# A cross-attention kernel: Wkv split by column halves in turn with the first context block, and x normalised behind the third piece

## Chip, cores and metric

The kernel runs on one core of one Trainium2 chip. The metric is device microseconds of one execution; the median of several runs is compared. The profile is that of one execution of its own.

## What is computed

A block of a perceiver on x (8 x 64 x 512) and a context (8 x 1601 x 512): cross-attention, a second attention whose values are taken on the diagonal, and a mixture of eight experts. The change touches only the start of the cross-attention. Its reference, cut:

```python
q = (x @ Wq + bq).reshape(B, N, H, hd).transpose(0, 2, 1, 3)
kv = (ctx @ Wkv + bkv).reshape(B, K, 2, H, hd).transpose(2, 0, 3, 1, 4)
k, v = (kv[0], kv[1])
attn = jnp.einsum('bhnd,bhkd->bhnk', q * SCALE, k)
attn = jax.nn.softmax(attn, axis=-1)
out = jnp.einsum('bhnk,bhkd->bhnd', attn, v)
...
return out @ Wproj + bproj
...
x = x + _L0_xattn_ref(_layernorm(x, axis=-1), ctx_1024, ...)
```

## The kernel before

Every engine's program is written out by hand and in order; they wait for each other with semaphores alone. A product in single precision is made of three: each operand is split into a high part (ScalarE copies it to fp32r, names in `_hi`) and a low part (VectorE subtracts the high part from the whole, `_lo`), and TensorE adds high x high, high x low and low x high in one bank (function `three`, lines 151 to 153). A "piece" is one bank of keys or values, 12 such matmuls over the four quarters k of the 512 rows of Wkv.

A unit works on half the context of one batch (a chunk of 7 or 6 tiles of 128 rows). While it attends, it makes the keys and values of the next unit. The first unit has nothing to attend to, and its preparation stands by itself ahead of the loops; the change lies there. It runs as follows.

SyncE issues all loads on one queue: the first four tiles of context (`raw0`, 1 MB), four quarters of Wkv of 512 KB (each with a semaphore of its own, `wkv_in0` to `wkv_in3`), the bias of the keys `bkc` (2 KB, semaphore `bk_in`), x, Wq, the bias of q, and three more tiles of context. The next load of context waits for `turned` to be 4, the one behind it for 12.

TensorE turns the context in four quarters (line 693, semaphore `turned`), waits for all of `cT_lo` (`turn_lo`) and all of `Wkv_lo` (`wkv_lo`), and makes eight pieces (n = 0 to 7: four of keys, four of values) in three banks in rotation. From n = 3 on each waits until VectorE has split the piece that was in its bank (`kv_lo`). Behind n = 4 and 5 it turns the normalised x (`turn_x`, line 706, waits for `ln_done`), behind n = 6 and 7 the second part of the context (line 665); then it makes q in four pieces (waits for `wq_lo`), then seven more pieces with turns of the next chunk. q is split, written to DRAM and read back by heads before the first scores (line 756).

ScalarE's and VectorE's orders match: four quarters of context, four quarters of Wkv (full width, 1024 columns), pieces 0 and 1, the normalisation of x (VectorE has the statistics, `norm_vector`, lines 113 to 139; ScalarE the square root in between, `norm_scalar`), pieces 2 and 3, Wq, and so on. A keys' piece is two instructions on each engine, a values' piece one. Both engines wait for `bk_in` ahead of their first copy. The argument `between` of `norm_vector` puts other work into VectorE's wait for the root.

Of the kernel before, what the change touches and what calls it, by code (L numbers as in the profile page):

```python
# [24 lines left out]
def perceiver_kernel(nc, x_in, ctx_in, Wq, bq, Wkv, bkv, Wproj, bproj,  # L25
                     WQ, WK, WVd, WVu, Wg, bg, W1, b1, W2, b2, out):
    B, S, D = x_in.shape
# [36 lines left out]
    with ExitStack() as whole:  # L64
# [241 lines left out]
        def program(block):  # L306
# [93 lines left out]
            def _(act):  # L400
# [25 lines left out]
                def first_kv_hi(n):  # L426
                    kv_hi(n, first_kv_bank(n), 0, n)

                act.wait_ge(sem("bk_in"), 16)
                for k in range(KC):  # L430
                    first_ctx_hi(k, 0, 0, k)
                for k in range(KC):
                    act.wait_ge(sem(f"wkv_in{k}"), 16)
                    nc.scalar.copy(Wkv_hi[:, k, :], Wkv_raw[:, k, :]).then_inc(sem("wkv_hi"), 1)
                first_kv_hi(0)
                first_kv_hi(1)
                norm_scalar(act, 1, lnt1)
                first_kv_hi(2)
                first_kv_hi(3)
                act.wait_ge(sem("wq_in"), 16)  # L440
# [6 lines left out]
                first_kv_hi(4)  # L447
                x_hi(0)
                x_hi(1)
                first_kv_hi(5)  # L450
                x_hi(2)
                x_hi(3)
                first_kv_hi(6)
                first_ctx_hi(2 * KC + 0, 0, 1, 0)
                first_ctx_hi(2 * KC + 1, 0, 1, 1)
                first_kv_hi(7)
# [58 lines left out]
            def _(dve):  # L515
# [32 lines left out]
                dve.wait_ge(sem("bk_in"), 16)  # L548
                for k in range(KC):
                    first_ctx_lo(k, 0, 0, k)  # L550
                for k in range(KC):
                    dve.wait_ge(sem("wkv_hi"), k + 1)
                    nc.vector.tensor_tensor(Wkv_lo[:, k, :], Wkv_raw[:, k, :], f32(Wkv_hi[:, k, :]), ALU.subtract) \  # L553
                        .then_inc(sem("wkv_lo"), 1)
                first_kv_lo(0)
                first_kv_lo(1)
                dve.wait_ge(sem("x_in"), 16)
                norm_vector(dve, 1, x_tok, x_tok, lnt1)
                first_kv_lo(2)
                first_kv_lo(3)  # L560
                dve.wait_ge(sem("wq_hi"), 1)
                nc.vector.tensor_tensor(Wq_lo[:, :, :], Wq_raw[:, :, :], f32(Wq_hi[:, :, :]), ALU.subtract) \
                    .then_inc(sem("wq_lo"), 1)
# [6 lines left out]
                first_kv_lo(4)  # L570
                x_lo(0)
                x_lo(1)
                first_kv_lo(5)
                x_lo(2)
                x_lo(3)
                first_kv_lo(6)
                first_ctx_lo(2 * KC + 0, 0, 1, 0)
                first_ctx_lo(2 * KC + 1, 0, 1, 1)
                first_kv_lo(7)
# [77 lines left out]
            def _(pe):  # L657
# [53 lines left out]
                pe.wait_ge(sem("turn_lo"), KC)  # L711
                pe.wait_ge(sem("wkv_lo"), KC)
                for n in range(8):
                    if n >= 3:
                        pe.wait_ge(sem("kv_lo"), n - 2 if n < 7 else n - 1)
# [1368 lines left out]
```

## Time and profile before

| | |
|---|---|
| median of 3 runs | 1428.68 us (1428.05 to 1432.59) |
| profiled execution | 1433.56 us |
| its span (first to last instruction) | 1431.5 us |
| busy: TensorE, VectorE, ScalarE, GpSimd | 1331.0, 937.2, 759.0, 101.6 us |
| mean granted TensorE clock | 0.974 |

TensorE is busy for nearly the whole span. The chain that ended last, followed back from the last instruction, tells on which engine time would have to be saved. Of the time before the loops (up to 82.3 us of the profiled execution) the timeline tells what each engine did and, in square brackets, how long it had stood idle and what released it. The granted clock is a share of 2.4 GHz.

### The profile page before, as it was taken

The numbers are of one execution on the slowest core, as the hardware profiler recorded it, in microseconds if no ns is written. First come the engines' busy times: TensorE is split into PE (matmuls) and PEld (weight loads), VectorE is DVE, ScalarE is ACT, GpSimd is POOL, SyncE is SP. The second block draws the span as 40 slices with busy tenths as digits, with TensorE's granted clock in tenths as the row PEclk, the third lists the DMA queues.
The fourth block names the chain that finished last, engine by engine and source line by source line (L and its number), as shares of the span: only waits on it lengthen the run. The fifth ranks groups of instructions, "written<-read, shape, count | busy, mean of one in ns | idle before, by whom it ended". The sixth has DMA issues, their size and how long they took to land.

```text
span 1431.5 us, 21997 instructions
## 1 busy us (share of the span) xinstructions
PE 1331.0 (93%) x7407; PEld 1151.9 (80%) x7408; DVE 937.2 (65%) x1498; ACT 759.0 (53%) x1320; POOL 101.6 (7%) x75
## 2 busy tenths in 40 slices
PE   5999999999999999999999999956898799999995
PEld 4888888899889889888898889845777577878774
DVE  3666666667567666666666666648489836578772
ACT  3455565566556555555555555533332526578770
POOL 0000000000000000000000000063243120000001
PEclk9999999999999999999999999977899899999997
DMA  5121011110101112112101110570548357399983
GB/s 191 55 71 49 27 44 44 33 44 22 52 19 50 29 33 59 29 29 60 33 26 44 44 33 16 105 176 16 106 122 305 130 198 257 133 338 343 341 284 96
DMA packets 129443, 146.15 MB, mean 102 GB/s; under 512 B 66408, under 2 KB 69864, under 8 KB 129392
## 3 DMA queue, kind: packets, MB, share of 16 engines
q1 hardware_dynamic: 128128, 141.49, 32.1%
q0 software_dynamic: 1280, 4.20, 0.9%
q8 instruction: 21, 0.34, 0.1%
q14 instruction: 14, 0.11, 0.0%
HBM read 125.02 MB, written 20.12 MB: 101 GB/s over the span
## 4 chain that ended last, share of the span: by engine, by line
PE 70%; DVE 14%; issue 6%; DMA 5%; ACT 4%; SPq 1%; DVEq 0%; POOL 0%; ACTq 0%; POOLq 0%
PE ps_scores L151 12%; PE ps_scores L153 12%; PE ps_scores L152 12%; PE ps_out L779 6%; PE ps_turn L767 5%; PE ps_scores L756 5%; PE ps_turn L665 2%; DVE stat L621 2%; PE ps_scores L2009 2%; PE ps_scores L2007 2%; PE ps_scores L2008 2%; DMA wu_raw<-in_L_ffn_W_dram 2%; DMA b1rows<-b_parts 2%; DVE Ks L531 2%; DVE wu_lo L1903 1%
## 5 line engine op out<-in xcount | busy, mean ns | idle before, releaser
L531 DVE SCALAR_TENSOR_TENSOR Ks<-ps_scores,bkc,Ks 64x384 fp32r<-64x384 f32 (+2 forms) x254 | 160.5, 632 | 147.9 <-ACT Ks L415 144.8
L151 PE MATMUL ps_scores<-cT_hi,Wkv_hi 128*128 128x384 f32 (+2 forms) x508 | 184.6, 363 | 6.4 <-DVE Wkv_lo L553 6.4
L493 ACT ACTIVATE Pr<-ps_scores,stat 128x705 f32<-128x705 f32 (+1 forms) x128 | 119.6, 934 | 115.5 <-DVE stat L621 115.5
L153 PE MATMUL ps_scores<-cT_hi,Wkv_lo 128*128 128x384 f32 (+2 forms) x508 | 175.4, 345 | 0.0
L152 PE MATMUL ps_scores<-cT_lo,Wkv_hi 128*128 128x384 f32 (+2 forms) x508 | 175.0, 344 | 0.0
L415 ACT ACTIVATE Ks<-ps_scores,bkc 64x384 fp32r<-64x384 f32 (+2 forms) x254 | 149.6, 589 | 43.0 <-PE ps_scores L153 41.2
L151 PE MATMUL ps_scores<-Wkv_hi,cT_hi 128*128 128x512 f32 (+1 forms) x412 | 170.6, 414 | 0.5 <-DVE Ks L531 0.5
L480 ACT CAST PT<-ps_turn 128x512 fp32r<-128x512 f32 (+2 forms) x256 | 110.2, 483 | 110.4 <-PE ps_turn L767 109.6
L537 DVE TENSOR_TENSOR Vs<-ps_scores,Vs 128x512 fp32r<-128x512 f32 (+1 forms) x103 | 71.2, 691 | 148.9 <-ACT Vs L419 148.3
L153 PE MATMUL ps_scores<-Wkv_hi,cT_lo 128*128 128x512 f32 (+1 forms) x412 | 162.4, 394 | 0.0
L152 PE MATMUL ps_scores<-Wkv_lo,cT_hi 128*128 128x512 f32 (+1 forms) x412 | 161.8, 393 | 0.0
L779 PE MATMUL ps_out<-PT,Vs 128*128 128x256 f32 x832 | 124.6, 288 | 25.8 <-DVE PT L613 21.0
L779 PEld LDWEIGHTS ps_out<-PT,Vs 128*128 128x128 f32 x832 | 114.7, 191 | 37.7 <-DVE PT L613 25.1
L1903 DVE TENSOR_TENSOR wu_lo<-wu_raw,wu_hi 128x2048 fp32r<-128x2048 f32 x56 | 126.5, 2287 | 15.8 <-ACT wu_hi L1744 15.8
L419 ACT CAST Vs<-ps_scores 128x512 fp32r<-128x512 f32 (+1 forms) x103 | 60.4, 586 | 140.8 <-PE ps_scores L153 139.9
L609 DVE TENSOR_TENSOR PT<-ps_turn,PT 128x512 fp32r<-128x512 f32 (+2 forms) x256 | 130.0, 550 | 4.9 <-ACT PT L480 4.0
L621 DVE TENSOR_REDUCE stat<-ps_scores 128x1 f32<-128x705 f32 (+1 forms) x128 | 125.8, 983 | 6.7 <-DVE stats L642 3.4
L1744 ACT CAST wu_hi<-wu_raw 128x2048 fp32r<-128x2048 f32 x56 | 105.7, 1917 | 19.6 <-DMA wu_raw<-in_L_ffn_W_dram 18.7
L767 PE MATMUL ps_turn<-ident,Pr 128*128 128x128 f32 x832 | 113.5, 275 | 0.0
L151 PEld LDWEIGHTS ps_scores<-cT_hi,Wkv_hi 128*128 128x128 f32 x508 | 96.2, 189 | 11.2 <-issue 6.7
L767 PEld LDWEIGHTS ps_turn<-ident,Pr 128*128 128x128 f32 x832 | 99.8, 142 | 6.0
L153 PEld LDWEIGHTS ps_scores<-cT_hi,Wkv_lo 128*128 128x128 f32 x508 | 96.0, 189 | 5.6
(355 smaller groups left out, 2455.0 us busy)
## 6 DMA issues: line engine op xcount, KB each, us to landing
wu_raw<-in_L_ffn_W_dram SPq DMA_DIRECT2D x64, 1024.0 KB, 7.5
raw<-in_ctx_dram SPq DMA_DIRECT2D x16, 768.0 KB, 4.6
raw<-in_ctx_dram SPq DMA_DIRECT2D x8, 1024.0 KB, 5.3
raw<-in_ctx_dram SPq DMA_DIRECT2D x8, 512.0 KB
sorted_x<-zeros SPq DMA_DIRECT2D x1, 4096.0 KB, 15.1
sorted_out<-zeros SPq DMA_DIRECT2D x1, 4096.0 KB, 25.6
o_heads<-U SPq DMA_DIRECT2D x56, 64.0 KB, 1.7
oA<-o_heads SPq DMA_DIRECT2D x8, 448.0 KB, 9.4
```

What stands on the lines that cost most here:

```text
L151: nc.tensor.matmul(out_ap, sh, mh, start=(i == 0), stop=False)
L152: nc.tensor.matmul(out_ap, sh, ml, start=False, stop=False)
L153: last = nc.tensor.matmul(out_ap, sl, mh, start=False, stop=(i == len(pairs) - 1))
L415: ins = nc.scalar.activation(Ks[c][0:64, 2 * i + h, o:o + wide], acc[64 * h:64 * h + 64, 0:wide], ACT.Identity, bias=bkc[:, 2 * i + h:2 * ...
L480: ins = nc.scalar.copy(PT[:, full[0]:full[-1] + 1, 0, :], acc[:, 0:P * len(full)].rearrange("p (t r) -> p t r", r=P))
L493: nc.scalar.activation(Pr[:, i % 2, 0:VALID[c]], S_cols(c, 0, VALID[c]), ACT.Exp, bias=stat[:, 0, c, i:i + 1], accum_out=stat[:, 1, c, i:i ...
L531: ins = nc.vector.scalar_tensor_tensor(out=Ks[c][64:128, j, o:o + wide], in0=acc[64 * h:64 * h + 64, 0:wide], scalar=bkc[:, j:j + 1], in1= ...
L609: ins = nc.vector.tensor_tensor(PT[:, full[0]:full[-1] + 1, 1, :], acc[:, 0:P * len(full)].rearrange("p (t r) -> p t r", r=P), f32(PT[:, f ...
L621: nc.vector.tensor_reduce(stat[:, 0, c, i:i + 1], S_cols(c, 0, VALID[c]), AX.X, ALU.max, negate=True).then_inc(sem("s_max"), 1)
L767: ins = nc.tensor.matmul(bank(P_BANKS[q])[0:M, at:at + P], Pr[:, (i - 1) % 2, t * P:t * P + M], ident[:, :], is_transpose=True, start=True ...
L779: ins = nc.tensor.matmul(psO_heads, Vs[c][0:M, t, i - 1, :], PT[0:M, t, :, :].rearrange("p a r -> p (a r)"), start=(t == 0), stop=(t == CH ...
L1903: nc.vector.tensor_tensor(wu_lo[v][:, :, :], wu_raw[v % RING][:, :, :], f32(wu_hi[v][:, :, :]), ALU.subtract).then_inc(sem("wu_lo_done"), 1)
```

## The change

ScalarE and VectorE no longer split Wkv in full rows behind the context. They split the half with the keys' columns, quarter by quarter, in turn with the quarters of the context; the half with the values' columns follows in two parts, between pieces 0, 1 and 2. The wait for `bk_in` moves from the head of both engines to the first instruction that reads the bias. TensorE's first piece waits for each quarter of context and of Wkv by itself and not for all; its three matmuls per quarter are in another order, the sum is the same. It waits for the second half of Wkv ahead of the first piece of values. The normalisation of x moves on VectorE from behind piece 1 to behind piece 2, with the split of piece 3 in its gap for the root; on ScalarE the root is behind piece 3. The turns of x move from behind n = 4 and 5 to behind n = 5 and 6, those of the context from behind n = 6 and 7 to behind n = 7 and behind the first piece of q. VectorE's `Wq_lo` moves behind the first two quarters of x. Nothing is computed that was not computed before; each Wkv split is two instructions of 512 columns where it was one of 1024.

```diff
@@ -426,17 +426,24 @@
                 def first_kv_hi(n):
                     kv_hi(n, first_kv_bank(n), 0, n)
 
-                act.wait_ge(sem("bk_in"), 16)
+                def wkv_hi(half, k):
+                    cols = slice(D * half, D * half + D)
+                    act.wait_ge(sem(f"wkv_in{k}"), 16)
+                    nc.scalar.copy(Wkv_hi[:, k, cols], Wkv_raw[:, k, cols]).then_inc(sem("wkv_hi"), 1)
+
                 for k in range(KC):
                     first_ctx_hi(k, 0, 0, k)
-                for k in range(KC):
-                    act.wait_ge(sem(f"wkv_in{k}"), 16)
-                    nc.scalar.copy(Wkv_hi[:, k, :], Wkv_raw[:, k, :]).then_inc(sem("wkv_hi"), 1)
+                    wkv_hi(0, k)
+                act.wait_ge(sem("bk_in"), 16)
                 first_kv_hi(0)
+                wkv_hi(1, 0)
+                wkv_hi(1, 1)
                 first_kv_hi(1)
-                norm_scalar(act, 1, lnt1)
+                wkv_hi(1, 2)
+                wkv_hi(1, 3)
                 first_kv_hi(2)
                 first_kv_hi(3)
+                norm_scalar(act, 1, lnt1)
                 act.wait_ge(sem("wq_in"), 16)
                 nc.scalar.copy(Wq_hi[:, :, :], Wq_raw[:, :, :]).then_inc(sem("wq_hi"), 1)
 
@@ -445,15 +452,15 @@
                     nc.scalar.copy(xT_hi[:, k, :], first_turn_bank(KC + k)).then_inc(sem("turn_hi"), 1)
 
                 first_kv_hi(4)
+                first_kv_hi(5)
                 x_hi(0)
                 x_hi(1)
-                first_kv_hi(5)
+                first_kv_hi(6)
                 x_hi(2)
                 x_hi(3)
-                first_kv_hi(6)
+                first_kv_hi(7)
                 first_ctx_hi(2 * KC + 0, 0, 1, 0)
                 first_ctx_hi(2 * KC + 1, 0, 1, 1)
-                first_kv_hi(7)
                 first_ctx_hi(2 * KC + 2, 0, 1, 2)
                 first_ctx_hi(2 * KC + 3, 0, 1, 3)
                 for m in range(KC):
@@ -545,22 +552,25 @@
                 def first_kv_lo(n):
                     kv_lo(n, first_kv_bank(n), 0, n)
 
-                dve.wait_ge(sem("bk_in"), 16)
+                def wkv_lo(half, k):
+                    cols = slice(D * half, D * half + D)
+                    dve.wait_ge(sem("wkv_hi"), KC * half + k + 1)
+                    nc.vector.tensor_tensor(Wkv_lo[:, k, cols], Wkv_raw[:, k, cols], f32(Wkv_hi[:, k, cols]),
+                                            ALU.subtract).then_inc(sem("wkv_lo"), 1)
+
                 for k in range(KC):
                     first_ctx_lo(k, 0, 0, k)
-                for k in range(KC):
-                    dve.wait_ge(sem("wkv_hi"), k + 1)
-                    nc.vector.tensor_tensor(Wkv_lo[:, k, :], Wkv_raw[:, k, :], f32(Wkv_hi[:, k, :]), ALU.subtract) \
-                        .then_inc(sem("wkv_lo"), 1)
+                    wkv_lo(0, k)
+                dve.wait_ge(sem("bk_in"), 16)
                 first_kv_lo(0)
+                wkv_lo(1, 0)
+                wkv_lo(1, 1)
                 first_kv_lo(1)
+                wkv_lo(1, 2)
+                wkv_lo(1, 3)
+                first_kv_lo(2)
                 dve.wait_ge(sem("x_in"), 16)
-                norm_vector(dve, 1, x_tok, x_tok, lnt1)
-                first_kv_lo(2)
-                first_kv_lo(3)
-                dve.wait_ge(sem("wq_hi"), 1)
-                nc.vector.tensor_tensor(Wq_lo[:, :, :], Wq_raw[:, :, :], f32(Wq_hi[:, :, :]), ALU.subtract) \
-                    .then_inc(sem("wq_lo"), 1)
+                norm_vector(dve, 1, x_tok, x_tok, lnt1, between=lambda: first_kv_lo(3))
 
                 def x_lo(k):
                     dve.wait_ge(sem("turn_hi"), KC + k + 1)
@@ -568,15 +578,18 @@
                         .then_inc(sem("turn_lo"), 1)
 
                 first_kv_lo(4)
+                first_kv_lo(5)
                 x_lo(0)
                 x_lo(1)
-                first_kv_lo(5)
+                dve.wait_ge(sem("wq_hi"), 1)
+                nc.vector.tensor_tensor(Wq_lo[:, :, :], Wq_raw[:, :, :], f32(Wq_hi[:, :, :]), ALU.subtract) \
+                    .then_inc(sem("wq_lo"), 1)
+                first_kv_lo(6)
                 x_lo(2)
                 x_lo(3)
-                first_kv_lo(6)
+                first_kv_lo(7)
                 first_ctx_lo(2 * KC + 0, 0, 1, 0)
                 first_ctx_lo(2 * KC + 1, 0, 1, 1)
-                first_kv_lo(7)
                 first_ctx_lo(2 * KC + 2, 0, 1, 2)
                 first_ctx_lo(2 * KC + 3, 0, 1, 3)
                 dve.wait_ge(sem("bq_in"), 16)
@@ -708,26 +721,35 @@
                                                is_transpose=True, start=True, stop=True)
                     ins.then_inc(sem("turned"), 1)
 
-                pe.wait_ge(sem("turn_lo"), KC)
-                pe.wait_ge(sem("wkv_lo"), KC)
-                for n in range(8):
+                _, wide = sub_cols(0, 0)
+                for k in range(KC):
+                    pe.wait_ge(sem("turn_lo"), k + 1)
+                    pe.wait_ge(sem("wkv_lo"), k + 1)
+                    for n, (W, C) in enumerate(((Wkv_hi, cT_hi), (Wkv_lo, cT_hi), (Wkv_hi, cT_lo))):
+                        ins = nc.tensor.matmul(first_kv_bank(0)[:, 0:wide], W[:, k, 0:P], C[0][:, k, 0:wide],
+                                               start=(k == 0 and n == 0), stop=(k == KC - 1 and n == 2))
+                ins.then_inc(sem("kv_made"), 1)
+                for n in range(1, 8):
                     if n >= 3:
                         pe.wait_ge(sem("kv_lo"), n - 2 if n < 7 else n - 1)
+                    if n == KC:
+                        pe.wait_ge(sem("wkv_lo"), 2 * KC)
                     make_kv(first_kv_bank(n), 0, n)
-                    if n == 4:
+                    if n == 5:
                         turn_x(0)
                         turn_x(1)
-                    elif n == 5:
+                    elif n == 6:
                         turn_x(2)
                         turn_x(3)
-                    elif n == 6:
+                    elif n == 7:
                         first_turn_ctx(2 * KC + 0, 0, 1, 0)
                         first_turn_ctx(2 * KC + 1, 0, 1, 1)
-                    elif n == 7:
+                pe.wait_ge(sem("wq_lo"), 1)
+                pe.wait_ge(sem("turn_lo"), 2 * KC)
+                for m in range(KC):
+                    if m == 1:
                         first_turn_ctx(2 * KC + 2, 0, 1, 2)
                         first_turn_ctx(2 * KC + 3, 0, 1, 3)
-                pe.wait_ge(sem("wq_lo"), 1)
-                for m in range(KC):
                     if m == 3:
                         pe.wait_ge(sem("q_scaled"), 1)
                     cols = slice(m * P, (m + 1) * P)
```

On TensorE, the first matmuls of the program. Before, four turns of the last quarter of context (`ps_turn`), and then piece 0 (`ps_scores`), which waits once:

```order
L693 MATMUL ps_turn<-ident,raw_59 128x128 [waits turn_lo]
L693 MATMUL ps_turn<-ident,raw_59 128x128 x3
L151 MATMUL ps_scores<-cT_hi_57,Wkv_hi 128x512 [waits wkv_lo,turn_lo]
L152 MATMUL ps_scores<-cT_lo_58,Wkv_hi 128x512
L153 MATMUL ps_scores<-cT_hi_57,Wkv_lo 128x512
L151 MATMUL ps_scores<-cT_hi_57,Wkv_hi 128x512
```

The same place in the changed kernel:

```order
L706 MATMUL ps_turn<-ident,raw_59 128x128 [waits turn_lo]
L706 MATMUL ps_turn<-ident,raw_59 128x128 x3
L729 MATMUL ps_scores<-cT_hi_57,Wkv_hi 128x512 [waits wkv_lo,turn_lo]
L729 MATMUL ps_scores<-cT_hi_57,Wkv_lo 128x512
L729 MATMUL ps_scores<-cT_lo_58,Wkv_hi 128x512
L729 MATMUL ps_scores<-cT_hi_57,Wkv_hi 128x512 [waits wkv_lo,turn_lo]
```

Each quarter now has a wait of its own, so that three matmuls can run as soon as one quarter of both operands is split.

On VectorE, from the split of Wkv to the normalisation. Before (`Ks_53` are the keys, a pair of rows is one piece; `st_79` and what follows are the statistics of x):

```order
L553 TENSOR_TENSOR Wkv_lo<-Wkv_raw,Wkv_hi 128x1024 [waits wkv_hi] x4
L531 SCALAR_TENSOR_TENSOR Ks_53<-ps_scores,bkc,Ks_53 64x512 [waits kv_hi]
L531 SCALAR_TENSOR_TENSOR Ks_53<-ps_scores,bkc,Ks_53 64x512
L531 SCALAR_TENSOR_TENSOR Ks_53<-ps_out,bkc,Ks_53 64x512 [waits kv_hi]
L531 SCALAR_TENSOR_TENSOR Ks_53<-ps_out,bkc,Ks_53 64x512
L121 BN_STATS st_79<-x_tok 128x6 [waits x_in]
```

The changed kernel, from the last half of the keys' columns on:

```order
L558 TENSOR_TENSOR Wkv_lo<-Wkv_raw,Wkv_hi 128x512 [waits wkv_hi]
L538 SCALAR_TENSOR_TENSOR Ks_53<-ps_scores,bkc,Ks_53 64x512 [waits kv_hi,bk_in]
L538 SCALAR_TENSOR_TENSOR Ks_53<-ps_scores,bkc,Ks_53 64x512
L558 TENSOR_TENSOR Wkv_lo<-Wkv_raw,Wkv_hi 128x512 [waits wkv_hi] x2
L538 SCALAR_TENSOR_TENSOR Ks_53<-ps_out,bkc,Ks_53 64x512 [waits kv_hi]
L538 SCALAR_TENSOR_TENSOR Ks_53<-ps_out,bkc,Ks_53 64x512
L558 TENSOR_TENSOR Wkv_lo<-Wkv_raw,Wkv_hi 128x512 [waits wkv_hi] x2
L538 SCALAR_TENSOR_TENSOR Ks_53<-ps_scores,bkc,Ks_53 64x512 [waits kv_hi]
L538 SCALAR_TENSOR_TENSOR Ks_53<-ps_scores,bkc,Ks_53 64x512
L121 BN_STATS st_79<-x_tok 128x6 [waits x_in]
```

Four half splits and a third piece now stand between the first piece and the statistics; piece 3 follows inside the normalisation.

On TensorE, the difference behind the second piece of values (n = 5), where the turns of x (`x_tok`) stand:

```order
 L152 MATMUL ps_scores<-Wkv_lo,cT_hi_57 128x512
 L153 MATMUL ps_scores<-Wkv_hi,cT_lo_58 128x512
-L706 MATMUL ps_turn<-ident,x_tok 128x128 [waits turn_lo]
-L706 MATMUL ps_turn<-ident,x_tok 128x128 x3
-L706 MATMUL ps_turn<-ident,x_tok 128x128 [waits turn_lo]
-L706 MATMUL ps_turn<-ident,x_tok 128x128 x3
+L719 MATMUL ps_turn<-ident,x_tok 128x128 [waits turn_lo,ln_done]
+L719 MATMUL ps_turn<-ident,x_tok 128x128 x3
+L719 MATMUL ps_turn<-ident,x_tok 128x128 [waits turn_lo]
+L719 MATMUL ps_turn<-ident,x_tok 128x128 x3
 L151 MATMUL ps_scores<-Wkv_hi,cT_hi_57 128x512 [waits kv_lo]
 L152 MATMUL ps_scores<-Wkv_lo,cT_hi_57 128x512
```

Where the third and fourth quarter of x were turned, the first and second are turned now, with the wait for `ln_done` that stood one piece earlier.

## Rows read from the trace of the kernel before

**Rows 1.** The page: the span, and the chain by engine.

```profile
span 1431.5 us, 21997 instructions
...
PE 1331.0 (93%) x7407; PEld 1151.9 (80%) x7408; DVE 937.2 (65%) x1498; ACT 759.0 (53%) x1320; POOL 101.6 (7%) x75
...
PE 70%; DVE 14%; issue 6%; DMA 5%; ACT 4%; SPq 1%; DVEq 0%; POOL 0%; ACTq 0%; POOLq 0%
```

**Rows 2.** Timeline, 6 to 27 us: start, duration, instruction, [idle before, releaser].

```profile
6.40 2.79 PE L693 MATMUL ps_turn<-ident,raw 128*128 128x128 f32 x12 [6.40 <-DMA raw<-in_ctx_dram]
...
7.57 1.28 ACT L404 ACT_TABLE_LOAD   x1 [7.44 <-PE ps_turn L693]
...
11.99 1.56 ACT L404 CAST cT_hi<-ps_turn 128x512 fp32r<-128x512 f32 x3 [3.13 <-DMA bkc<-in_L_xattn_bkv_dram]
12.68 1.89 DVE L519 TENSOR_TENSOR cT_lo<-ps_turn,cT_hi 128x512 fp32r<-128x512 f32 x3 [12.56 <-ACT cT_hi L404]
...
13.43 1.12 PE L693 MATMUL ps_turn<-ident,raw 128*128 128x128 f32 x4 [4.24 <-DVE cT_lo L519]
...
15.06 3.88 ACT L434 CAST Wkv_hi<-Wkv_raw 128x1024 fp32r<-128x1024 f32 x4
...
16.14 4.63 DVE L553 TENSOR_TENSOR Wkv_lo<-Wkv_raw,Wkv_hi 128x1024 fp32r<-128x1024 f32 x4 [0.25 <-ACT Wkv_hi L434]
...
20.92 0.76 PE L151 MATMUL ps_scores<-cT_hi,Wkv_hi 128*128 128x512 f32 x1 [6.38 <-DVE Wkv_lo L553]
...
26.18 0.63 PE L151 MATMUL ps_out<-cT_hi,Wkv_hi 128*128 128x512 f32 x1
```

**Rows 3.** Chain in order of time, its first pieces: start, duration, what.

```profile
1.30 0.49 SPq L343
...
3.06 0.44 SPq L343
3.54 8.42 DMA bkc<-in_L_xattn_bkv_dram
```

**Rows 4.** Tile Wkv_raw: from issue to landing of its four loads.

```profile
DMA to landing us min/median/max: 6.2/7.4/8.7
```

**Rows 5.** DMA issues, 0 to 25 us: tile, count, KB each, us to landing.

```profile
x_tok<-in_x_dram SPq DMA_DIRECT2D x1, 1024.0 KB, 10.2
```

**Rows 6.** Timeline, 27 to 45 us, VectorE, ScalarE and TensorE.

```profile
27.83 1.51 DVE L531 SCALAR_TENSOR_TENSOR Ks<-ps_scores,bkc,Ks 64x512 fp32r<-64x512 f32 x2 [7.06 <-ACT Ks L415]
...
29.57 1.39 ACT L415 ACTIVATE Ks<-ps_out,bkc 64x512 fp32r<-64x512 f32 x2 [1.77 <-PE ps_out L153]
...
30.99 1.51 DVE L531 SCALAR_TENSOR_TENSOR Ks<-ps_out,bkc,Ks 64x512 fp32r<-64x512 f32 x2 [1.64 <-ACT Ks L415]
...
32.53 2.48 DVE L121 BATCH_NORM_STATS2 st<-x_tok 128x6 f32<-128x512 f32 x4
...
35.45 0.17 DVE L126 TENSOR_SCALAR ve<-mv 128x4 f32<-128x4 f32 x1
...
35.90 0.18 DVE L131 RECIPROCAL rt<-rt 128x4 f32<-128x4 f32 x1 [0.27 <-ACT rt L145]
...
36.91 1.92 DVE L137 TENSOR_SCALAR x_tok<-x_tok,mv,rs 128x512 f32<-128x512 f32 x4
...
38.88 1.09 PE L706 MATMUL ps_turn<-ident,x_tok 128*128 128x128 f32 x8 [1.19 <-DVE x_tok L137]
...
40.42 0.58 PE L151 MATMUL ps_scores<-Wkv_hi,cT_hi 128*128 128x512 f32 x1 [0.45 <-DVE Ks L531]
...
44.86 0.60 PE L706 MATMUL ps_turn<-ident,x_tok 128*128 128x128 f32 x4
```

**Rows 7.** Busy time in stretches: length, each engine with count, granted clock, DMA.

```profile
26.80:37.70 10.90, 10.89 (x48) 8.60 (x46) 7.65 (x20) 5.62 (x9) 0.00 (x0) 1.00 0.00 0
...
40.50:44.00 3.50, 3.50 (x9) 2.73 (x10) 3.46 (x3) 1.56 (x3) 0.00 (x0) 0.53 0.02 5
```

**Rows 8.** Timeline, 64 to 83 us: VectorE's split of q, and the first scores.

```profile
64.73 2.49 DVE L589 TENSOR_TENSOR q_lo<-q_sb,q_hi 128x512 fp32r<-128x512 f32 x4
...
82.32 0.67 PE L756 MATMUL ps_scores<-Ks,Qs_hi 128*128 128x448 f32 x2 [0.29 <-ACTq L468]
```

## The prediction

> **What bounds the kernel now.** The profile's page first: TensorE is busy 93% of the span and holds 70% of the chain that ended last [rows 1]. A kernel like that gets shorter where TensorE stands still, so I read the start in order of time. TensorE turns the first context block from 6.40 us and makes its first keys only at 20.92 us [rows 2]. Both gaps in between have one origin. ScalarE's first copy is queued behind the wait for the bias `bkc`, a 2 KB transfer that was queued behind four pieces of Wkv and landed at 3.54 + 8.42 = 11.96 us [rows 3]; the copy starts at 11.99 and ran against a quarter turned long before. Then ScalarE copies all four quarters of context before any of Wkv, and VectorE ends Wkv_lo at 16.14 + 4.63 = 20.77 us [rows 2].
>
> From 20.92 us on TensorE is the bound with one exception: the turn of normalised x starts at 38.88 us after 1.19 us of idleness, and 0.45 us more pass before the next piece at 40.42 us, which waits for a bank that VectorE empties late, behind the normalisation [rows 6]. Behind that the chain is TensorE's up to the first scores at 82.32 us, where it stands 0.29 us [rows 8]. Every later wait is on work of this chain and none on a time of day, so what is won before 82 us reaches the end.
>
> Call the keys' pieces K0 to K3 and the values' V0 to V3 (n = 0 to 7).
>
> **The clock.** The twelve matmuls of K0 take 26.18 - 20.92 = 5.26 us, 0.44 us each [rows 2], which is the 1.2 GHz level for 512 columns; 48 records in 10.90 us, 0.227 us each, stand behind 26.8 us, the 2.4 GHz level [rows 7]. A warm piece costs 12 x 0.227 = 2.72 us. After the idleness ahead of and behind the turn of x the granted clock reads 0.53 for 3.5 us [rows 7], and the piece from 40.42 to 44.86 us took 4.44 us [rows 6], 1.72 us over a warm one.
>
> **Step 1, the first keys.** Without the bias wait ScalarE starts when the first quarter is turned: the table load saw it at 7.44 us [rows 2], so 7.45 instead of 11.99 us. The chain from ScalarE's copy to VectorE's is 0.69 us (11.99 to 12.68) and to the fourth turn 1.44 (11.99 to 13.43); it gives 8.9 us, earlier than TensorE is done with the first twelve turns (9.19). The fourth quarter then ends at 9.19 + 1.12 = 10.3 us [rows 2]. Wkv's quarters land between 1.30 + 6.2 = 7.5 us and 3.06 + 8.7 = 11.8 us [rows 3, 4]. The halves cost about 0.55 us on ScalarE (four full ones are 3.88 us, half of 0.97 plus some), and 0.62 us on VectorE (2.49 / 4, the same form in q_lo [rows 8]); four pairs on VectorE from 8.15 us are 4 x (0.63 + 0.62) = 5.0 us, 13.15 us, and by the last landing 11.8 + 0.6 + 0.1 + 0.65 = 13.15 us too. TensorE at the low level needs 5.26 us for K0 from 10.3 us, so its own pace binds: 15.6 us for 26.2 before. Its floor, when the clock is up early, is 13.15 + 3 x 0.43 = 14.4 us. K0 is therefore 10.6 us early.
>
> **Step 2, where the stall goes.** VectorE is next late. Before, its part of K0 started at 27.83 us, 1.65 us behind the first matmul of K1 (26.18 us) [rows 2, 6]; now that is 15.6 + 1.65 = 17.25 us. Behind it stand, in its queue, two keys' pieces of 1.50 us each, four half Wkv_lo (4 x 0.62 = 2.5 us, full ones before cost 4.63 for the whole matrix and lay ahead of K0), K2 (1.50), statistics (32.53 to 35.62, 3.1 us), K3 (1.50), and the rest of the normalisation (35.90 to 38.83, 2.95 us) [rows 6]. 1.5 x 4 + 2.5 + 3.1 + 2.95 = 14.55 us, so x is ready at 31.8 us, or later by what VectorE waits for K1. K1: the clock rose 26.8 - 20.92 = 5.9 us after matmuls began; I take the same delay, from 10.3 to 16.2 us. ScalarE then takes K1 up as before 29.57 - 26.18 = 3.4 us behind its first matmul, at 19.0 us, and VectorE 1.42 us later (29.57 to 30.99) [rows 6], at 20.4 us. VectorE is free at 17.25 + 1.5 + 1.25 = 20.0 us, so it waits 0.4 us. x is ready and its turn starts at 32.2 us, for 38.88 before: 6.7 us early.
>
> TensorE meanwhile ends K0 at 15.6, K1 at 18.8 and then a piece each 2.72 us: K2 21.5, K3 24.2, V0 27.0, V1 29.7 us (V0's wait for all of Wkv_lo ends at 23.2 us, V1's for the bank of K2 at 24.7). It idles 29.7 to 32.2 = 2.5 us, where it idled 1.19. But V1 is now ahead of the turn, 2.72 us of work done, and K3's split no longer holds the next piece (its values wait for kv_lo 4, over at 29.3 us): 0.45 us. The table load (1.28 us) and root hide behind K3's split.
>
> VectorE's waits behind x: V0, V1, two halves of x, then Wq_lo (2.3 us) at about 34.5 to 36.8 us; V3 needs only V1's split, the context turns need x's, and Q0 starts near 43 us. TensorE is the later one by about 2 us or more at each, so I cost them at nothing; without that cover the moved Wq_lo would cost up to its 2.3 us. The two context turns moved behind Q0 change the order and not the sum. SyncE's load of the next block waits for four turned quarters and goes out at 10.3 instead of about 14.6 us, behind x and Wq in the queue; x landed at 4.35 + 10.2 = 14.6 us [rows 5], long before 24 us.
>
> **Sum.** 6.7 + 2.72 + 0.45 = 9.9 us, if the low clock behind the turn of x costs the 1.72 us that it did. The profiled execution took 1433.56 us with a span of 1431.5 us; it would be 1423.7 and 1421.6. The median of the runs is 1428.68, 4.9 us below that execution: 1418.8 us.
>
> **Two rules against it.** [rows 7] show TensorE at 1.2 GHz after it stood still, and at 2.4 GHz only after it had worked. The Trainium skill, TensorE: Matmul & The Clock Gate, Part 1, says the low level is the default and activity releases it. The trace agrees (26.8 and 40.5 us). By its rule, working in quarters and a longer stall could keep the clock low for longer; that is rival 1. On the halves, a full Wkv_lo is 4.63 / 4 = 1.16 us and two halves 2 x 0.62, so that splitting costs 0.08 us each, 0.3 us in all [rows 2, 8]. The Trainium skill, VectorE: DVE Perf Modes, on the TRN2 errata, gives a fixed cost for each instruction of about 150 cycles, an estimate of 0.16 us at its 0.96 GHz; by that the four added ones would be 0.6 us. The rows decide.
>
> **Rivals.**
> 1. The clock stays low longer. A matmul costs 0.43 - 0.227 = 0.2 us more. If it rises 3.5 us later in K0 and K1, K1 ends 1.7 us later, and x with it (VectorE waits for K1); if the 2.5 us of idleness and the turns give two low stretches instead of one, 1.7 us more. The gain is then 5 to 7 us: 1422.7 us. For it: the stall doubles. Against: the quarters leave TensorE no gap, since it is slower than its supply. The mirror case, a stall that costs no low stretch, gives 11.7 us: 1417.
> 2. VectorE becomes the bound through the whole first unit, not only up to x. If Wq_lo, V2 and x's last halves run one behind the other after a late x, Q0 waits up to 2.3 us and with rival 1 the gain falls under 4.3 us: 1425.5.
> 3. The head is hidden anyway: the first scores wait for the round trip of q or for context loads. For it: at 82.32 us the wait is on ScalarE's queue. Against: it is 0.29 us [rows 8], and q's stores and loads hang on Q3, which moves with the rest. It would give 1428.7.
> 4. Slower: the clock does not rise at all while TensorE is fed at the pace of VectorE. Ahead of the scores stand 19 pieces of 12 matmuls, 228; it needs 50 more of them at the low level (10 us / 0.2 us) to lose the gain, and 75 to be over 4.3 us slower, 1433. Nothing in [rows 7] shows a low stretch over 6 us while pieces stand behind each other.
>
> **Numbers.** 0.3% is 4.3 us, about what a measurement of this kernel can tell from no change. The forecast, 8 to 12.5 us gained, 0.70; rival 1 short of that (4.3 to 8 us) 0.14; rivals 2 and 3 0.12; rival 4 0.04. All above 4.3 us is faster: 0.84, 0.12 within, 0.04 slower. The forecast's own range is 1416 to 1421; runs of one kernel lay 4.5 us apart, so with rival 1 and a part of 2 the range is 1414.5 to 1425.
>
> **What would show it.** Right: ScalarE's first copy at 7.5 us, first keys at 10.3, K0 done by 15.6, x turned at 32.2, a stall of 2 to 3 us ahead of it with V1 before, first scores at 72.3 us. Wrong: first keys past 11 us (landing of Wkv), a granted clock near 0.5 for more than 3.5 us behind 32 us, TensorE idle ahead of Q0, or the ten microseconds lost behind 72 us.

## The result, and the profile after

Over 8 runs of each, the changed kernel took 1418.29 us in the median (1415.79 to 1425.5) and the kernel before 1430.83 us (1428.05 to 1434.62). The ratio is 0.9917, with a 95% interval of 0.9897 to 0.9937: 11.9 us less (9.0 to 14.7); the two medians themselves differ by 12.5 us. The forecast was 1418.8 us in a range of 1414.5 to 1425.0, a gain of 9.9 us. One execution each of experiments 3 and 6 took 2222 and 1909 us, at a mean granted clock of 0.557 and 0.649, and no figure below uses them.

The page of the profile after (its execution took 1417.58 us), lines that answer to [rows 1]:

```profile
span 1415.7 us, 22010 instructions
...
PE 71%; DVE 14%; issue 6%; DMA 4%; ACT 3%; SPq 1%; DVEq 0%; POOL 0%; ACTq 0%; POOLq 0%
```

The page alone says little. The span is 15.8 us shorter, more than the runs are. The timeline of the changed kernel at its head, which answers to [rows 2], tells where it was won:

```profile
0.79 1.28 ACT L404 ACT_TABLE_LOAD   x1 [0.66 <-PEq L2093]
...
6.35 3.65 PE L706 MATMUL ps_turn<-ident,raw 128*128 128x128 f32 x16 [6.35 <-DMA raw<-in_ctx_dram]
7.47 0.58 ACT L404 CAST cT_hi<-ps_turn 128x512 fp32r<-128x512 f32 x1 [5.40 <-PE ps_turn L706]
7.96 0.62 ACT L432 CAST Wkv_hi<-Wkv_raw 128x512 fp32r<-128x512 f32 x1
...
9.65 0.78 PE L729 MATMUL ps_scores<-cT_hi,Wkv_hi 128*128 128x512 f32 x1
...
10.65 0.44 PE L729 MATMUL ps_scores<-cT_lo,Wkv_hi 128*128 128x512 f32 x1
...
10.93 0.39 PE L729 MATMUL ps_scores<-cT_hi,Wkv_hi 128*128 128x512 f32 x1
...
11.86 0.62 ACT L432 CAST Wkv_hi<-Wkv_raw 128x512 fp32r<-128x512 f32 x1 [0.67 <-DMA Wkv_raw<-in_L_xattn_Wkv_dram]
...
12.51 0.69 DVE L558 TENSOR_TENSOR Wkv_lo<-Wkv_raw,Wkv_hi 128x512 fp32r<-128x512 f32 x1
...
13.35 0.47 PE L729 MATMUL ps_scores<-cT_hi,Wkv_hi 128*128 128x512 f32 x1 [0.49 <-DVE Wkv_lo L558]
```

ScalarE starts at 7.47 us and its copies of context and Wkv alternate; the first keys start at 9.65 us. The spacing of TensorE's rows falls at 10.9 us from 0.43 to 0.23 us, and from then on TensorE is faster than its supply: the last quarter is late by Wkv's landing at 11.86 us, over ScalarE and VectorE. ScalarE's table load, which stood at 7.57 us before [rows 2], is at 0.79 us now.

The granted clock does not show that rise. The stretch in which the matmuls start 0.43 us apart reads (the clock is the third number from the end):

```profile
9.65:10.90 1.25, 1.25 (x5) 1.00 (x4) 1.25 (x3) 1.24 (x3) 0.00 (x0) 1.00 1.12 324
```

It reads 1.00 in the kernel before as well, from 20.9 to 26.8 us, where K0's matmuls are 0.43 us apart. So at the head I tell the level by the spacing, 0.43 us for the lower and 0.23 us for the upper. Behind 30 us the two agree.

The same timeline where it answers to [rows 6] and [rows 8]:

```profile
15.89 1.51 DVE L538 SCALAR_TENSOR_TENSOR Ks<-ps_scores,bkc,Ks 64x512 fp32r<-64x512 f32 x2 [2.69 <-ACT Ks L415]
17.44 1.29 DVE L558 TENSOR_TENSOR Wkv_lo<-Wkv_raw,Wkv_hi 128x512 fp32r<-128x512 f32 x2
...
26.30 1.51 DVE L538 SCALAR_TENSOR_TENSOR Ks<-ps_scores,bkc,Ks 64x512 fp32r<-64x512 f32 x2
...
28.85 1.91 DVE L137 TENSOR_SCALAR x_tok<-x_tok,mv,rs 128x512 f32<-128x512 f32 x4
...
30.82 1.65 PE L719 MATMUL ps_turn<-ident,x_tok 128*128 128x128 f32 x8 [2.91 <-DVE x_tok L137]
32.13 0.77 PE L151 MATMUL ps_scores<-Wkv_hi,cT_hi 128*128 128x512 f32 x1
...
36.13 1.04 PE L719 MATMUL ps_turn<-ident,x_tok 128*128 128x128 f32 x8
36.92 0.48 PE L151 MATMUL ps_scores<-Wkv_hi,cT_hi 128*128 128x512 f32 x1
...
70.49 0.67 PE L778 MATMUL ps_scores<-Ks,Qs_hi 128*128 128x448 f32 x2 [0.29 <-ACTq L475]
```

VectorE is busy without a gap from 15.89 us to the end of x at 30.76 us, and TensorE idles 2.91 us for it; the piece behind takes 4.00 us (32.13 to 36.13). Part of it is at the lower clock:

```profile
30.90:36.10 5.20, 5.20 (x20) 4.39 (x21) 4.77 (x5) 1.17 (x2) 0.00 (x0) 0.67 0.00 0
```

The first scores come at 70.49 us, 11.83 us before the 82.32 of [rows 8]. That is the gain of the runs. The remaining 4.0 us of the two spans lie behind the first scores, where both programs are the same: from there to the end the kernel before took 1349.2 us and this one 1345.2. In the ten other traces of this study that stretch has from 1345 to 1354 us, and the profiled execution of the kernel before was 2.7 us above the median of its runs, that of the changed kernel 0.7 us below. So most of those 4 us is the scatter of single executions. I therefore read each experiment at the first scores, where the two traces of the changed kernel agree within 0.3 us and the two of experiment 7 within 0.05 us, and take the runs as the check: in each experiment the gain read there lies inside the interval of the runs.

### The profile page after: what moved, and what is told of

Read it like the earlier page. It is cut to its first block, busy times and chain, and to the rows that moved or that the text cites. A ratio compares the mean times of both kernels' runs of the same rounds, so it can differ in the third digit from the quotient of the medians.

```text
span 1415.7 us, 22010 instructions
## 1 busy us (share of the span) xinstructions
PE 1326.8 (94%) x7407; PEld 1150.0 (81%) x7408; DVE 937.9 (66%) x1502; ACT 759.5 (54%) x1324; POOL 102.0 (7%) x75
## 4 chain that ended last, share of the span: by engine, by line
PE 71%; DVE 14%; issue 6%; DMA 4%; ACT 3%; SPq 1%; DVEq 0%; POOL 0%; ACTq 0%; POOLq 0%
PE ps_scores L151 12%; PE ps_scores L153 12%; PE ps_scores L152 12%; PE ps_out L801 6%; PE ps_turn L789 5%; PE ps_scores L778 5%; DMA b1rows<-b_parts 2%; PE ps_turn L678 2%; PE ps_scores L2031 2%; PE ps_scores L2029 2%; PE ps_scores L2030 2%; DVE stat L634 2%; DVE Ks L538 2%; DVE wu_lo L1925 2%; PE ps_out L2052 1%
## 5 line engine op out<-in xcount | busy, mean ns | idle before, releaser
L152 PEld LDWEIGHTS ps_scores<-cT_lo,Wkv_hi 128*128 128x128 f32 x504 | 95.1, 189 | 4.0
## 6 DMA issues: line engine op xcount, KB each, us to landing
sorted_x<-zeros SPq DMA_DIRECT2D x1, 4096.0 KB, 15.6
```

What stands on the lines that cost most here:

```text
L152: nc.tensor.matmul(out_ap, sh, ml, start=False, stop=False)
```

## The experiments

Gains at the first scores are against 82.32 us, and "runs" is the ratio to the kernel before with its interval. Each experiment has one trace, unless two are named.

**1. The bias wait alone.** The kernel before, with only this (the same on VectorE):

```diff
-                act.wait_ge(sem("bk_in"), 16)
                 for k in range(KC):
                     first_ctx_hi(k, 0, 0, k)
...
+                act.wait_ge(sem("bk_in"), 16)
                 first_kv_hi(0)
```

> The kernel before with one edit, the wait for the bias of the keys moved to its first reader. My theory (the head is a chain of ScalarE and VectorE, and the order of the splits behind the bias wait is worth as much as the wait): ScalarE starts at 7.5 us, ends the context's four quarters at about 10.7 and Wkv's four full rows at 14.6, VectorE ends at 16.4, first keys at 16.5 us for 20.92 before; 4.4 us gained, first scores at 77.9 us. Rival A (the bias wait is the whole gain): 10 us or more. Rival B (it only matters with the new order): under 1 us.

Measured: first keys at 16.44 us, first scores at 76.91 us, 5.4 us gained; runs 0.9952 [0.9936, 0.9969]. Its timeline, TensorE:

```profile
33.49 1.09 PE L706 MATMUL ps_turn<-ident,x_tok 128*128 128x128 f32 x8 [1.18 <-DVE x_tok L137]
...
35.03 0.50 PE L151 MATMUL ps_scores<-Wkv_hi,cT_hi 128*128 128x512 f32 x1 [0.45 <-DVE Ks L531]
...
37.89 0.60 PE L706 MATMUL ps_turn<-ident,x_tok 128*128 128x128 f32 x4
40.22 0.66 PE L706 MATMUL ps_turn<-ident,x_tok 128*128 128x128 f32 x4 [1.73 <-DVE xT_lo L567]
```

The chain of splits is as worked out, to 0.1 us. The idleness ahead of x is the same 1.18 us as before, yet no low clock follows: the piece takes 2.86 us (35.03 to 37.89) for 4.44. That would be 1.6 us more of gain, and a new wait takes it back: the turn at 40.22 us stood 1.73 us for VectorE, where the long Wq_lo lies ahead of x's halves. So taking away the wait for 2 KB is by itself worth 5.4 of the 11.8 us, and neither rival A nor B holds.

**2. The bias wait back at the head of the changed kernel.**

```diff
+                act.wait_ge(sem("bk_in"), 16)
                 for k in range(KC):
                     first_ctx_hi(k, 0, 0, k)
                     wkv_hi(0, k)
-                act.wait_ge(sem("bk_in"), 16)
                 first_kv_hi(0)
```

> The changed kernel with the wait for the bias put back at the head of ScalarE and VectorE. My theory: ScalarE starts at 12.0, the last split of the keys' half is done at 17.6, first keys start at 14.4 and end at 18.5 to 19.7 us for 14.1; 4.4 to 5.6 us later than the changed kernel, 6 to 7.5 us faster than before. Rival A (the bias wait is the whole gain): no faster than before by more than 2 us. Rival B (the order alone is the gain): within 1 us of the changed kernel.

Measured: first keys at 14.14 us, K1 from 18.43, x turned at 34.98 for 30.82 us, 4.2 us later, but first scores at 72.96 us, only 2.5 us later for the 4.4 to 5.6 expected; 9.4 us gained; runs 0.9941 [0.9922, 0.996]. The head went as expected, and the size was missed behind it. Its timeline:

```profile
34.98 1.10 PE L719 MATMUL ps_turn<-ident,x_tok 128*128 128x128 f32 x8 [2.79 <-DVE x_tok L137]
...
38.67 1.04 PE L719 MATMUL ps_turn<-ident,x_tok 128*128 128x128 f32 x8
```

From turn to turn it is 3.69 us, in the changed kernel 5.31 us (30.82 to 36.13). A stall of 2.79 us was followed by no low clock here; one of 2.91 us was there. The 1.6 us between these two are what separates 4.2 from 2.5 us. The parts of the change do not add up, then: the wait is worth 5.4 us when it alone is taken from the kernel before, and 2.5 us when it is put back into the changed one.

**3. All quarters at once.** The changed kernel, with TensorE's first piece waiting as before:

```diff
+                pe.wait_ge(sem("turn_lo"), KC)
+                pe.wait_ge(sem("wkv_lo"), KC)
                 for k in range(KC):
-                    pe.wait_ge(sem("turn_lo"), k + 1)
-                    pe.wait_ge(sem("wkv_lo"), k + 1)
```

> The changed kernel, but TensorE's first piece waits for all four quarters at once as before. My theory: it starts at 13.25 us and ends at 16.0 (clock up) to 18.5 us (clock low) for 14.1; VectorE's chain to x follows it, so x is turned 1.9 to 4.4 us later than 30.8 us and the first scores come that much later than 70.5 us. Rival (VectorE is the bound to x, and the quarters' waits are hidden by it): first scores within 0.5 us of 70.5.

Measured: first scores at 74.76 us, 4.3 us later; x turned at 35.08; runs 0.9945 [0.9926, 0.9964]. Its timeline, TensorE:

```profile
13.34 0.77 PE L729 MATMUL ps_scores<-cT_hi,Wkv_hi 128*128 128x512 f32 x1 [3.34 <-DVE Wkv_lo L558]
...
35.08 1.92 PE L719 MATMUL ps_turn<-ident,x_tok 128*128 128x128 f32 x8 [2.89 <-DVE x_tok L137]
```

TensorE stood 3.34 us, and the eleven matmuls behind that were about 0.43 us apart up to 18.15 us; K1 starts at 18.38 us for 14.1. In the changed kernel, which has no such pause, the clock was up by 11 us. The rival falls: VectorE's chain hangs on K0 and hides nothing. Two things are in the 4.3 us: nine of K0's matmuls that the changed kernel has done by 13.35 us, 2.0 us at the upper level, and some 2.2 us because all of K0 ran at the lower one here.

**4. x at its old place.** The changed kernel with the normalisation behind piece 1 and the turns of x behind n = 4 and 5, as before, with ScalarE's order to match; Wq_lo stays where the change put it. The edit in part:

```diff
-                first_kv_lo(2)
                 dve.wait_ge(sem("x_in"), 16)
-                norm_vector(dve, 1, x_tok, x_tok, lnt1, between=lambda: first_kv_lo(3))
+                norm_vector(dve, 1, x_tok, x_tok, lnt1)
+                first_kv_lo(2)
+                first_kv_lo(3)
...
-                    if n == 5:
+                    if n == 4:
                         turn_x(0)
                         turn_x(1)
```

> The changed kernel, but x is normalised behind the second piece and turned behind the first two pieces of values, as before. My theory: x is ready at 28.0 instead of 30.8 us, TensorE idles from 25.2 us, and the next piece waits for its bank until 29.5 us and runs partly at the low clock; the first scores come 0.5 to 1.5 us later than 70.5 us, so moving x is worth about 1 us of the 12. Rival (the move is worth the piece that it puts ahead of the turn): 2.7 us or more later.

Measured: x turned at 27.67 us after 2.65 us of idleness, first scores at 70.55 us, 0.06 us later; runs 0.9915 [0.99, 0.9929]. TensorE's next piece starts at 29.21 us after a wait of 0.45 us for its bank and lasts to 33.50, at the low clock for a part:

```profile
27.67 1.09 PE L720 MATMUL ps_turn<-ident,x_tok 128*128 128x128 f32 x8 [2.65 <-DVE x_tok L137]
29.21 0.80 PE L151 MATMUL ps_scores<-Wkv_hi,cT_hi 128*128 128x512 f32 x1 [0.45 <-DVE Ks L538]
```

So the part of the change that its name ends with is worth nothing that shows here: 2.72 us of work ahead of the turn, and the turn 3.15 us later. Both theories gave it too much.

**5. TensorE warmed ahead of the data.** The changed kernel, with turns that nobody reads:

```diff
                 pe.wait_ge(sem("ident_ready"), 1)
+                for i in range(20):
+                    nc.tensor.matmul(bank(0)[:, P * (i % 4):P * (i % 4) + P], ident[:, :], ident[:, :],
+                                     is_transpose=True, start=True, stop=True)
```

> The changed kernel with 20 turns of the identity into a bank that nobody reads, ahead of the first context turn (about 1.6 to 6.3 us). It tests what raises TensorE's clock and what the low clock costs at the head. If turns raise it as matmuls do: the context's turns start 0.11 us apart instead of 0.23 and the first keys are at 0.227 us each, but the last quarter still waits for Wkv's landing until 13.35 us, so the time is within 0.5 us of the changed kernel. If turns do not raise it: the rows of the head are as in the changed kernel.

Measured: first scores at 70.28 us (70.49 and 70.21 without); runs 0.9915 [0.9895, 0.9935]. Its timeline, TensorE:

```profile
1.58 4.53 PE L702 MATMUL ps_scores<-ident 128*128 128x128 f32 x20 [1.58 <-POOL ident L389]
6.24 1.75 PE L709 MATMUL ps_turn<-ident,raw 128*128 128x128 f32 x12
8.51 0.66 PE L709 MATMUL ps_turn<-ident,raw 128*128 128x128 f32 x4 [0.53 <-DVE cT_lo L526]
9.20 0.47 PE L732 MATMUL ps_scores<-cT_hi,Wkv_hi 128*128 128x512 f32 x1
...
13.22 0.47 PE L732 MATMUL ps_scores<-cT_hi,Wkv_hi 128*128 128x512 f32 x1 [0.69 <-DVE Wkv_lo L558]
```

Turns do raise the clock: 12 of the context take 1.75 us for the 2.79 of [rows 2], and K0 begins at the upper level (its first matmuls are 0.22 to 0.31 us apart), though TensorE had done nothing but turns. The Trainium skill, TensorE: Matmul & The Clock Gate, Part 4, says that the full clock does not engage for transposes; here the trace disagrees, and the measurement decides. It brings nothing, as expected, since the last quarter waits for its data until 13.22 us whatever the clock.

**6. The stall filled.** The changed kernel, ahead of the turn of x:

```diff
                     if n == 5:
+                        for i in range(12):
+                            nc.tensor.matmul(bank(1), Wkv_hi[:, i % KC, 0:P], cT_hi[0][:, i % KC, :],
+                                             start=True, stop=True)
                         turn_x(0)
```

> The changed kernel with 12 products of data that are there into a bank that nobody reads, in TensorE's stall ahead of the turn of x (2.72 us of 2.91). If the stall costs a low stretch of the clock behind it: no low stretch, the turn of x takes 0.9 instead of 1.3 us and the next piece 2.72 instead of 4.00, 1.7 us faster than the changed kernel. Rival (the clock behind the stall costs nothing that is not hidden, VectorE being late): within 0.3 us.

> The changed kernel with the 12 filler products once more, for its trace. If the stall costs a low stretch: the turn of x in 1.1 us or less, the next piece in 2.72 us for 4.00, no granted clock under 1.00 between 27 and 40 us, first scores at 68.8 us for 70.5. If not: first scores at 70.2 to 70.5 us.

Measured: runs 0.9897 [0.9882, 0.9912]; in the trace of the second the first scores are at 68.74 us, 1.75 us before the changed kernel (1.47 us before its other trace, experiment 9). Its timeline, and the stretch behind it (the granted clock is the third number from the end):

```profile
30.76 1.09 PE L719 MATMUL ps_turn<-ident,x_tok 128*128 128x128 f32 x8 [0.19 <-DVE x_tok L137]
```

```profile
30.00:34.00 4.00, 3.81 (x22) 2.97 (x21) 3.92 (x7) 1.08 (x2) 0.00 (x0) 1.00 0.00 0
```

x is no earlier, TensorE does 2.72 us of useless work, and yet the first scores come earlier. From the first turn of x to the second it takes 3.69 us (30.76 to 34.45), and 5.31 us in both traces of the changed kernel: the low stretch behind the stall costs 1.6 us, where the forecast had 1.72. The runs point the same way, but their interval overlaps with that of the changed kernel.

**7. VectorE's chain shortened.** The values' half of Wkv is split ahead of piece 0, in the idleness there; the four statistics of x stand behind pieces 0 and 1, where the half splits stood; the root comes ahead of piece 3 on ScalarE, and piece 3's split behind the normalisation. VectorE's order, without the definition of `x_stats` (ScalarE's answers to it):

```diff
                 for k in range(KC):
                     first_ctx_lo(k, 0, 0, k)
                     wkv_lo(0, k)
+                for k in range(KC):
+                    wkv_lo(1, k)
                 dve.wait_ge(sem("bk_in"), 16)
                 first_kv_lo(0)
-                wkv_lo(1, 0)
-                wkv_lo(1, 1)
-                first_kv_lo(1)
-                wkv_lo(1, 2)
-                wkv_lo(1, 3)
-                first_kv_lo(2)
                 dve.wait_ge(sem("x_in"), 16)
-                norm_vector(dve, 1, x_tok, x_tok, lnt1, between=lambda: first_kv_lo(3))
+                x_stats(0)
+                x_stats(1)
+                first_kv_lo(1)
+                x_stats(2)
+                norm_vector(dve, 1, x_tok, x_tok, lnt1, last_stats=lambda: x_stats(3), between=lambda: first_kv_lo(2))
+                first_kv_lo(3)
```

> The changed kernel with VectorE's chain to x made shorter: the values' half of Wkv split ahead of the first piece, in the idleness there, the statistics of x in the gaps behind pieces 0 and 1, the root ahead of piece 3 on ScalarE, and piece 3's split behind the normalisation. My theory (VectorE's queue is what x waits for): x is ready at 26.5 to 28 us, TensorE does not idle ahead of its turn, no low clock behind; 4 to 4.6 us faster than the changed kernel, first scores at 66 us. Rival (TensorE's own pieces or ScalarE's bind soon after): 1 us or less.

> The kernel with the statistics in the gaps once more, beside the one that loads Wkv by halves. First scores at 65.4 to 65.9 us and no low clock between 27 and 40 us, if that follows from the missing stall and was no luck of one execution; 1414 to 1416 us.

Measured: first scores at 65.65 and 65.60 us, 4.8 us before the changed kernel and 16.7 before the first; runs 0.9879 [0.9862, 0.9896] and 0.9894 [0.9873, 0.9914], medians 1414.95 and 1416.02 us. The first trace, VectorE and TensorE:

```profile
15.97 1.51 DVE L538 SCALAR_TENSOR_TENSOR Ks<-ps_scores,bkc,Ks 64x512 fp32r<-64x512 f32 x2 [0.35 <-ACT Ks L417]
17.51 1.29 DVE L571 BATCH_NORM_STATS2 st<-x_tok 128x6 f32<-128x512 f32 x2
...
24.84 1.92 DVE L139 TENSOR_SCALAR x_tok<-x_tok,mv,rs 128x512 f32<-128x512 f32 x4
...
26.80 1.51 DVE L538 SCALAR_TENSOR_TENSOR Ks<-ps_scores,bkc,Ks 64x512 fp32r<-64x512 f32 x2
...
27.72 1.03 PE L724 MATMUL ps_turn<-ident,x_tok 128*128 128x128 f32 x8
```

VectorE's 2.69 us of idleness ahead of piece 0 have become 0.35. x is ready at 26.76 us, TensorE comes to its turn at 27.72 with no idle time in front of it, and in both traces the granted clock is 1.00 from 27 to 40 us. The turn starts 3.1 us earlier, of which 2.91 are the stall, and from turn to turn it takes 1.7 us less, the low stretch; that is the gain. From its first split to x VectorE takes 10.8 us for 14.9. Of these 4.1 us, 2.6 are the half splits moved into the idleness, and 1.5 are piece 3's split, which starts at 26.80 us, behind x, and stood inside the normalisation at 26.30 us in the changed kernel. The two were moved together, and no run has one without the other.

**8. Wkv's landing.** The kernel of 7, with Wkv loaded by halves:

```diff
-                for k in range(KC):
-                    sp.dma_start(Wkv_raw[:, k, :], wkv[:, k, :]).then_inc(sem(f"wkv_in{k}"), 16)
+                for half in range(2):
+                    for k in range(KC):
+                        cols = slice(D * half, D * half + D)
+                        sp.dma_start(Wkv_raw[:, k, cols], wkv[:, k, cols]).then_inc(sem(f"wkv_in{half}{k}"), 16)
```

> The kernel with the statistics in the gaps, and Wkv loaded by halves too, the keys' half of all four quarters first, each with a semaphore of its own. In the kernel with the gaps used the last three matmuls of K0 wait for the last quarter's landing (start at 13.36 us). If the landing binds the head: they start with VectorE's eighth split at 12.85 us, and everything behind comes 0.5 us earlier, first scores at 65.1 us for 65.65. Rival (the smaller transfers and four more issues cost as much): first scores at 65.6 us or later, or x landing late enough to hold VectorE's statistics at 17.5 us.

Measured: first scores at 65.61 us, the last quarter of K0 from 13.27 us; runs 0.9885 [0.9865, 0.9905]. ScalarE no longer waits for a landing, but VectorE starts 0.13 us later than in the second trace of 7 (8.23 for 8.10 us, with the context's own landing) and has eight operations of 0.60 us; it would be done by 13.0 us anyway. The 0.5 us expected did not come. Landing and VectorE were level, and I had counted the gain from VectorE's start in another trace.

**9. The changed kernel again.**

> The changed kernel once more, for a second trace of it. If the moment at which the clock rises depends on the execution and not on the program: first matmuls again at 9.65 us but the rise elsewhere than 10.9 us (up to 3.4 us later), first keys done up to 1.5 us later, and the time 1415 to 1420 us. If it is the program's: the rise within 0.2 us of 10.9 us.

Measured: 1419.45 us (1415.5 to 1423.73), runs 0.9913 [0.9895, 0.9932]; first matmuls at 9.53 us, the clock up at 10.3 us, x turned at 30.59 us behind 2.91 us of idleness, a low stretch behind it again, first scores at 70.21 us. The rise moved by 0.6 us, more than the 0.2 that would have made it the program's. Experiments 4 and 6 have the same head up to there, and it is at 11.8 and 11.7 us; experiment 7, the same again, had it before its first matmul at 9.47 us in one trace and at 10.4 us in the other. So it is the execution's.

## Why the prediction was right, point by point

**What bounds.** Right. TensorE was the bound except for the head and the turn of x; both can be moved, and 11.8 us at the first scores became 11.9 us in the runs. Rival 3 is out: the wait at the first scores is 0.29 us in every trace ([rows 8] and the row at 70.49 us above), though they came up to 17 us earlier.

**Step 1.** Right that the bias wait and the order of the splits made the head late, short in size. First keys at 9.65 us for 10.3: I had given the last four turns the 1.12 us that they take by themselves, and added it to the end of the twelve before; in a row, sixteen take 6.35 to 9.65 us, 0.21 us each. K1 starts at 14.1 us for 15.6. The step let the clock rise 5.9 us behind the first matmul, as it did before, and it rose 1.3 us behind it. "Its own pace binds" was wrong there: K0 ended at the pace of Wkv's last landing and its splits, and that did not hang on the exact moment of the rise (at 11.8 and 11.7 us in experiments 4 and 6, with K1 at 13.9 and 14.1 us). The floor of 14.4 us was too high, as it took 0.43 us for each of the last three matmuls though the clock was to be up; they took 0.78 us together. Experiment 3 shows what the quarters' waits are worth, 4.3 us, and experiment 1 that the bias wait alone brings 5.4.

ScalarE's start, 7.47 us for 7.45, was luck in part. Before, the table load stood between the first turn and ScalarE's first copy, from 7.57 us for 1.28 us [rows 2], and step 1 put the copy at 7.45 us without a price for it. By these rows it would have started at 8.85 us, 1.4 us later (an estimate). The load is at 0.79 us in every trace without the bias wait at the head, and at 7.54 us in experiment 2, which has it. So it moved with the wait, and the forecast did not see that it had to.

**Step 2.** The sum came out, in part by two misses that cancel: it had 14.55 us of work from piece 0's split to x and 0.4 us of waiting for K1; measured were 14.9 us of work (15.89 to 30.76) and no wait. x is turned at 30.82 us for 32.2, 1.4 us earlier by step 1 alone. The stall ahead of it was 2.91 us for 2.5.

**The sum.** 9.9 us forecast, 11.83 us at the first scores. The turn of x came 8.06 us earlier (38.88 to 30.82) for 6.7, that is 1.4 us of step 1. The turn itself and what followed up to the next piece took 1.31 us for 1.54, where 0.45 of gain was forecast: the turn ran slower than before. The piece behind it gave 0.44 us (4.00 for 4.44). The third and fourth quarter of x gave 0.37 us that I did not list: before, they took 1.16 us, since the fourth waited for VectorE's split of a quarter before it, and now 0.79 us (36.13 to 36.92). Their rows before:

```profile
45.61 0.66 PE L706 MATMUL ps_turn<-ident,x_tok 128*128 128x128 f32 x4
46.02 0.48 PE L151 MATMUL ps_scores<-Wkv_hi,cT_hi 128*128 128x512 f32 x1
```

From there to the first scores TensorE has one piece less to do, 2.73 us for 2.72. Together 8.06 + 0.23 + 0.44 + 0.37 + 2.73 = 11.83 us. It lies near the 11.7 us of rival 1's mirror case, but not by its mechanism: the low stretch was there. The 0.45 us for the bank is gone as forecast. What was credited to V1 ahead of the turn, 2.72 us, is arithmetic of the two timelines and no gain of the move: with x at its old place (experiment 4) the turn comes 11.2 us earlier than before instead of 8.06, no piece is ahead of it, and the first scores are 0.06 us later. The step named a difference and not a cause.

**The rivals.** Rival 1 did not come: at the head the clock came up earlier, not later, and behind the turn there was one low stretch, as the sum had assumed; experiment 6 prices it at 1.6 us for 1.72. Rival 2 did not come: TensorE has no idle time between the turn of x and the 0.29 us at the first scores, and VectorE stood up to 2.0 us for it there. Rival 4 did not come: from 10.9 us on the matmuls are 0.23 us apart, but for the one low stretch. On the halves, the row decided rightly: two halves measured 1.29 us in a pair, where one full row took 1.22 us, so the split costs 0.07 us and not the 0.16 us estimated from the Trainium skill, VectorE: DVE Perf Modes, on the TRN2 errata.

**The span.** The two profiled spans differ by 15.8 us; 4.0 of them lie behind the first scores, and the runs do not show them. Whoever had read the traces alone would have found a third too much.

## What to carry to other kernels

A small load that a whole engine waits for belongs with its first reader: 2 KB at the head of two queues cost 5.4 us in the kernel before (experiment 1). Where a stall goes, look for what the next engine does in the idleness ahead of it: VectorE stood 2.69 us with work at hand. Moving that work there, together with piece 3's split out of the normalisation, was worth 4.8 us, while moving x behind another piece was worth none. To take a part out of a finished change and run it tells what it was worth; the difference of two timelines does not.

## What the runs showed of the hardware

The moment at which TensorE's clock rises is not the program's: in six traces with the same head it is before 9.5, at 10.3, 10.4, 10.9, 11.7 and 11.8 us. Whether a stall is followed by a low stretch does not follow from its length alone in these traces: behind 2.65 us (experiment 4), 2.89 (experiment 3), 2.90 (experiment 5) and 2.91 us (both traces of the changed kernel) there was one, behind 2.79 us (experiment 2) there was none; and the kernel before had one behind 1.19 and 0.45 us where experiment 1 had none behind 1.18 and 0.45 us. A low stretch there cost 1.6 us. At the head the granted clock reads 1.00 also where matmuls of 512 columns are 0.43 us apart (9.65 to 10.90 us in the changed kernel). Turns of 128 x 128 raised the clock without any product ahead of them (experiment 5). ScalarE's table load of 1.28 us is at 0.79 us in all traces but two: in the kernel before and in experiment 2, which wait for the bias at the head, it is behind the first turn, at 7.57 and 7.54 us. From the first scores to the end, with the same instructions, the traces scatter from 1345 to 1354 us.
